# Norms between the first projections, one step-size chain for eight tokens, scans moved one projection forward

## What is computed

```python
h = rmsnorm(hidden_states, ln1_w)
zxbcdt = h @ w_in.T                       # z 512, xs 128, B 128, C 512, dt 4 columns
z, xs, Bs, Cs, dt = split(zxbcdt)
xBC = silu(causal_conv4(concat(xs, Bs, Cs)) + conv_b)
dt = softplus(dt + dt_bias)               # the step size, 4 heads
a = dt * -exp(A_log)
Ldec = tril(exp(cumsum(a)[:, None] - cumsum(a)[None, :]))
att = (C @ B.T) * Ldec
Y = att @ (xs * dt) + D * xs              # one chunk of 128 positions, state starts at 0
out = hidden + (Y * silu(z)) @ w_out.T    # then rmsnorm, MLP, and the other blocks
```

## Time and profile before

| | us |
|---|---|
| median of 3 runs | 1008.77 |
| lowest, highest | 1008.63, 1014.3 |
| the profiled execution as a whole | 1011.68 |
| its span in the profile | 1009.8 |
| PE busy | 966.8 |
| DVE, ACT, POOL busy | 571.8, 496.7, 403.9 |

### The profile page before, as it was taken

How to read it: one execution, slowest core, us unless ns; L and a number is a source line. 1 busy time by engine, 2 the same in 40 slices (tenths; PEclk the granted TensorE clock), 3 DMA queues, 4 the chain that set the end, 5 groups by cost and what they waited for, 6 DMA issues and landing times.

```text
span 1009.8 us, 15358 instructions
## 1 busy us (share of the span) xinstructions
PE 966.8 (96%) x5010; PEld 806.4 (80%) x5010; DVE 571.8 (57%) x1338; ACT 496.7 (49%) x1374; POOL 403.9 (40%) x341
## 2 busy tenths in 40 slices
PE   5999899999999999899999999999999999999894
PEld 3866488878888887788888888888888888888781
DVE  3665553422221266666666666566666666666766
ACT  4655342422231346455655654655555555655455
POOL 4334633744343453342442532622623514523312
PEclk9999999999999999899999999999999999999997
DMA  6200013310111111010020020020010110100002
GB/s 217 82 3 32 11 52 118 105 63 0 62 62 62 61 45 55 22 48 38 21 83 0 21 83 0 21 83 0 28 76 0 62 42 1 61 0 0 1 1 84
DMA packets 12976, 45.60 MB, mean 45 GB/s; under 512 B 1616, under 2 KB 2256, under 8 KB 9872
## 3 DMA queue, kind: packets, MB, share of 16 engines
q1 hardware_dynamic: 12944, 45.20, 12.9%
HBM read 43.10 MB, written 2.10 MB: 45 GB/s over the span
## 4 chain that ended last, share of the span: by engine, by line
PE 86%; DVE 5%; POOL 3%; ACT 3%; issue 2%; DMA 1%; SPq 0%; DVEq 0%; ACTq 0%; POOLq 0%
PE bank L373 25%; PE bank L374 24%; PE bank L375 24%; PE bank L651 6%; PE bank L661 3%; PE bank L384 1%; POOL res L1430 1%; DVE cbuf L1630 1%; DVE bst L1767 1%; PE bank L638 1%; POOL h_lo L1321 1%; DMA res<-in_x 1%; PE bank L452 1%; DVE xn L1590 0%; POOL rstd L1325 0%
## 5 line engine op out<-in xcount | busy, mean ns | idle before, releaser
L373 PE MATMUL bank<-act_hi,w_hi 128*128 128x512 f32 x560 | 225.0, 402 | 2.0 <-DVE act_lo L1577 1.6
L374 PE MATMUL bank<-act_lo,w_hi 128*128 128x512 f32 x560 | 220.1, 393 | 0.0
L375 PE MATMUL bank<-act_hi,w_lo 128*128 128x512 f32 x560 | 220.0, 393 | 0.0
L1501 POOL TENSOR_TENSOR pb<-pb,prec 128x512 f32<-128x512 f32 x64 | 66.6, 1040 | 313.2 <-DVE prec L1902 313.2
L1156 ACT ACTIVATE pb<-pb,nmax 128x128 f32<-128x128 f32 x256 | 99.8, 391 | 77.6 <-DVE nmax L1897 77.6
L373 PEld LDWEIGHTS bank<-act_hi,w_hi 128*128 128x128 f32 x560 | 106.0, 189 | 25.6 <-issue 4.3
L375 PEld LDWEIGHTS bank<-act_hi,w_lo 128*128 128x128 f32 x560 | 106.1, 189 | 22.9
L374 PEld LDWEIGHTS bank<-act_lo,w_hi 128*128 128x128 f32 x560 | 106.2, 190 | 22.6 <-issue 1.4
L373 PE MATMUL bank<-w_hi,ot_hi 128*128 128x512 f32 x256 | 105.5, 412 | 0.8 <-DVE res L1915 0.8
L375 PE MATMUL bank<-w_hi,ot_lo 128*128 128x512 f32 x256 | 101.1, 395 | 0.0
L374 PE MATMUL bank<-w_lo,ot_hi 128*128 128x512 f32 x256 | 100.7, 393 | 0.0
(11 more groups left out here) (189 smaller groups left out, 2068.2 us busy)
## 6 DMA issues: line engine op xcount, KB each, us to landing
raw_a<-in_w_q SPq DMA_DIRECT2D x8, 1024.0 KB, 4.7
raw_b<-in_w_o SPq DMA_DIRECT2D x8, 1024.0 KB, 4.7
raw_a<-in_w_gu SPq DMA_DIRECT2D x7, 1024.0 KB, 5.2
raw_b<-in_w_kv SPq DMA_DIRECT2D x8, 512.0 KB, 3.3
raw_b<-in_w_dn SPq DMA_DIRECT2D x7, 512.0 KB, 3.5
res<-in_x SPq DMA_DIRECT2D x8, 256.0 KB, 6.3
raw_b<-in_ctx_t SPq DMA_DIRECT2D x8, 256.0 KB, 3.0
xre<-in_x SPq DMA_DIRECT2D x2, 1024.0 KB, 7.0
```

The source lines that it names most:

```text
L373: mm(o, l_hi, r_hi, start=first, stop=False)
L374: mm(o, l_hi, r_lo, start=False, stop=False)
L375: return mm(o, l_lo, r_hi, start=False, stop=last)
L1501: TT(pb[:, jj % 2, :, :], pb[:, jj % 2, :, :], prec[:, jj % 2, :].unsqueeze(2).to_broadcast([P, GH, L]), ALU.mult).then_inc(p_norm, 1)
```

## The change

1. **Norms of tokens 4 to 7.** `norm_t(4)` to `norm_t(7)` stood before `in_step(6)` to `in_step(9)` and now stand before `in_step(1)` to `in_step(4)`; `dt_step(1)` comes behind `in_step(4)`, before `in_step(5)` (it stood behind `in_step(9)`). ACT, DVE and POOL get their steps of these norms earlier; on POOL `diag_d` moves behind `win_rest(7)`.
2. **One step-size chain.** `dt_row` holds all 1024 positions, `sp` all 32 columns. There is one `dt_turn` with eight transposes, one `dt_in`, one `dt_exp`, one `dt_out`, on 128x32 elements for 128x16. `decay_in(b)` waits for this one chain.
3. **Scans earlier.** `ssm1` is split into `cum_step` (the sum along the positions) and `xs_step` (transposition and scores), in this order. All scans stand one projection earlier on PE; for tokens 4 to 7 the `cum_step`s stand among `in_step(15)` to `in_step(19)`. On DVE `att_mul(b)` comes ahead of a `conv`, `y_out(b - 1)` behind it, and for tokens 4 to 7 `add_res`, `rms_var` and `rms_x` come behind an `att_mul` and `y_out`. ACT and POOL follow (`decay(4)` and (5) before `in_evac(16)`, `decay(6)` and (7) ahead of `gu_hi(0, 1)`).

The core of the diff, PE's list first:

```diff
                 if f == 12:
-                    pe.wait_ge(dt_a, 2)
+                    pe.wait_ge(dt_a, 1)
...
                 if n:
-                    pe.wait_ge(dt_a, 1)
+                    pe.wait_ge(dt_ev, 1)
...
-            def dt_turn(n):
-
-                pe.wait_ge(dt_ev, n + 1)
-                for j in range(HALF):
-                    t = nc.tensor.transpose(bank[6][:, j * NH:(j + 1) * NH], dt_row[:, j * L:(j + 1) * L],
+            def dt_turn():
+
+                pe.wait_ge(dt_ev, 2)
+                for b in range(B):
+                    t = nc.tensor.transpose(bank[6][:, b * NH:(b + 1) * NH], dt_row[:, b * L:(b + 1) * L],
                                             ident[0:NH, 0:NH])
                 t.then_inc(dt_t, 1)
 
-            def ssm1(b):
+            def cum_step(b):
+
+                pe.wait_ge(md_done, b + 1)
+                pe.wait_ge(*((exp_done, b) if b else (n_lo, 8)))
+                mm(bank[2][:, :], strict, md[:, b % 2, :, :], start=True, stop=True).then_inc(cum_mm, 1)
+
+            def xs_step(b):
...
+            def ssm1(b):
+
+                cum_step(b)
+                xs_step(b)
...
             in_step(0)
             dt_step(0)
-            in_step(1)
-            dt_turn(0)
-            for f in range(2, 6):
-                in_step(f)
             for i in range(4, 8):
                 norm_t(i, (bank[2], bank[3]))
-                in_step(i + 2)
+                in_step(i - 3)
             dt_step(1)
+            in_step(5)
+            dt_turn()
+            for f in range(6, 10):
+                in_step(f)
+            ssm1(0)
             in_step(10)
-            dt_turn(1)
-            ssm1(0)
+            ssm1(1)
             in_step(11)
-            ssm1(1)
-            in_step(12)
             ssm2(0)
             ssm1(2)
-            in_step(13)
+            in_step(12)
             ssm2(1)
             ssm1(3)
+            in_step(13)
+            ssm2(2)
             in_step(14)
-            ssm2(2)
+            ssm2(3)
+            cum_step(4)
             in_step(15)
-            ssm2(3)
+            cum_step(5)
             in_step(16)
             in_step(17)
+            xs_step(4)
             in_step(18)
+            xs_step(5)
+            ssm2(4)
+            cum_step(6)
             in_step(19)
-            ssm1(4)
             pe.wait_ge(conv_c, 2 * NCONV)
             out_step(0)
-            ssm1(5)
-            ssm2(4)
+            ssm2(5)
+            cum_step(7)
+            xs_step(6)
             out_step(1)
-            ssm1(6)
-            ssm2(5)
+            xs_step(7)
+            ssm2(6)
             out_step(2)
-            ssm1(7)
-            ssm2(6)
+            ssm2(7)
             out_step(3)
-            ssm2(7)
```

ACT, from the first scan to the second norm:

```diff
             conv_silu(6)
-            in_evac(12)
+            in_evac(11)
             conv_silu(7)
             x_evac(2)
             decay(2)
             y_split(0)
-            in_evac(13)
+            in_evac(12)
             x_evac(3)
             decay(3)
             conv_silu(8)
...
             gu_hi(0, 0)
+            decay(6)
+            y_split(4)
             square(8)
-            y_split(4)
+            decay(7)
             x_evac(6)
-            decay(6)
+            y_split(5)
             gu_hi(0, 1)
             square(9)
```

DVE:

```diff
+            rms_var(4)
+            rms_var(5)
+            rms_x(4)
             conv(0)
...
+            conv(2)
             norm_lo(6, nb)
-            dt_out(0)
+            conv(3)
             norm_lo(7, nb)
+            conv(4)
+            dt_in()
+            conv(5)
+            dt_out()
+            att_mul(0)
             conv(6)
-            dt_in(1)
-            att_mul(0)
+            att_mul(1)
             conv(7)
-            att_mul(1)
             y_out(0)
-            dt_out(1)
+            att_mul(2)
             conv(8)
-            att_mul(2)
             y_out(1)
+            att_mul(3)
             conv(9)
-            att_mul(3)
             y_out(2)
             conv(10)
             y_out(3)
             conv(11)
-            add_res(0, 0, OUT_BANK[0])
             att_mul(4)
-            rms_var(8)
             att_mul(5)
             y_out(4)
+            add_res(0, 0, OUT_BANK[0])
+            rms_var(8)
+            att_mul(6)
+            y_out(5)
             add_res(1, 1, OUT_BANK[1])
+            att_mul(7)
+            y_out(6)
             rms_x(8)
             rms_var(9)
-            att_mul(6)
-            y_out(5)
             add_res(2, 2, OUT_BANK[2])
+            y_out(7)
             rms_x(9)
             rms_var(10)
-            att_mul(7)
-            y_out(6)
             add_res(3, 3, OUT_BANK[3])
-            y_out(7)
```

More of the change, by code:

```diff
@@ L80, in build_program @@
             dt_sb = sb(m, "dt_sb", [P, B * NH])
-            sp = sb(m, "sp", [P, 7, HALF * NH])
+            sp = sb(m, "sp", [P, 7, B * NH])
             cbuf = sb(m, "cbuf", [P, 3, NTOK])
             xbc = sb(m, "xbc", [P, 2, NCONV, NTOK])
-            dt_row = sb(m, "dt_row", [NH, NTOK])
+            dt_row = sb(m, "dt_row", [NH, B * L])
             diag_d = sb(m, "diag_d", [P, NH, L])
@@ L436, in ssm1 @@
                 nc.tensor.transpose(bank[7][:, 0:P], xbc[:, n, 0, tok], ident).then_inc(xt_mm, 1)
-                pe.wait_ge(md_done, b + 1)
-                if b:
-                    pe.wait_ge(exp_done, b)
-                mm(bank[2][:, :], strict, md[:, b % 2, :, :], start=True, stop=True).then_inc(cum_mm, 1)
                 if b >= 2:
@@ L884, in dt_evac, with dt_exp @@
                 act.wait_ge(dt_mm, n + 1)
-                if n:
-                    act.wait_ge(dt_t, n)
-                A(dt_row[:, :], bank[6][0:NH, :], ACT.Copy).then_inc(dt_ev, 1)
-            def dt_exp(n):
-                act.wait_ge(dt_a, n + 1)
+                A(dt_row[:, n * NTOK:(n + 1) * NTOK], bank[6][0:NH, :], ACT.Copy).then_inc(dt_ev, 1)
+            def dt_exp():
+                act.wait_ge(dt_a, 1)
                 A(sp[:, 2, :], sp[:, 1, :], ACT.Exp).then_inc(dt_exp_done, 1)
@@ L965, in _ @@
             conv_silu(8)
-            in_evac(14)
+            in_evac(13)
             y_split(1)
             conv_silu(9)
-            in_evac(15)
-            conv_silu(10)
+            in_evac(14)
             y_split(2)
@@ L981, in _ @@
             wout_hi(1)
+            decay(4)
+            in_evac(15)
+            decay(5)
+            conv_silu(10)
             conv_silu(11)
@@ L987, in _ @@
             in_evac(17)
+            x_evac(4)
             in_evac(18)
+            x_evac(5)
             in_evac(19)
-            x_evac(4)
-            decay(4)
-            x_evac(5)
-            decay(5)
             tb = (bank[0], bank[1])
@@ L1338, in _ @@
             win_rest(1)
+            win_rest(2)
+            rsqrt(4)
+            win_rest(3)
+            rsqrt(5)
+            win_rest(4)
+            rsqrt(6)
+            win_rest(5)
+            rsqrt(7)
+            win_rest(6)
+            win_rest(7)
             pool.wait_ge(ld_small[5], 16)
@@ L1345, in _ @@
             TT(qk_w[:, :], chan_sb[:, nq:nq + 1], chan_sb[:, nq + 1:nq + 2], ALU.mult).then_inc(setup_p, 1)
-            for p in range(2, 6):
-                win_rest(p)
+            win_rest(8)
+            win_rest(9)
             def decay_in(b):
-                pool.wait_ge(dt_done, b // HALF + 1)
+                pool.wait_ge(dt_done, 1)
                 if b == 0:
@@ L1366, in y_rest @@
                 lo(y_lo[:, b % 4, :, :], yb[:, b % 2, :, :], y_hi[:, b % 4, :, :], ylo_done)
-            for i in range(4, 8):
-                rsqrt(i)
-                win_rest(i + 2)
             decay_in(0)
@@ L1384, in _ @@
             y_rest(0)
+            decay_in(4)
             decay_out(3)
             y_rest(1)
-            decay_in(4)
+            decay_in(5)
             y_rest(2)
@@ L1390, in _ @@
             wout_rest(1)
-            decay_in(5)
+            decay_out(4)
+            decay_out(5)
             y_rest(3)
@@ L1394, in _ @@
             wout_rest(3)
+            decay_in(6)
+            decay_in(7)
             def gu_rest(c, i):
@@ L1404, in dn_rest @@
                 lo(w_lo[:, s], raw_b[:, i * 512:(i + 1) * 512], w_hi[:, s], dn_l)
-            decay_out(4)
-            decay_in(6)
-            decay_out(5)
-            decay_in(7)
             gu_rest(0, 0)
+            decay_out(6)
             y_rest(4)
-            decay_out(6)
+            decay_out(7)
             rsqrt(8)
             y_rest(5)
-            decay_out(7)
             gu_rest(0, 1)
             rsqrt(9)
-            gu_rest(0, 2)
             y_rest(6)
             rsqrt(10)
+            gu_rest(0, 2)
             y_rest(7)
@@ L1645, in dt_in, with dt_out @@
                 V.tensor_copy(sp[:, 1, :], sp[:, 3, :]).then_inc(dt_a, 1)
-            def dt_out(n):
-                dve.wait_ge(dt_exp_done, n + 1)
+            def dt_out():
+                dve.wait_ge(dt_exp_done, 1)
```

(11 more changed lines are left out.)

55 lines of the change are left out of this document (25 added, 30 removed).

## The result

| | before | after | ratio |
|---|---|---|---|
| median of 20 runs, us | 1012.93 | 1009.29 | 0.9973 (95%: 0.9961 to 0.9986) |
| lowest to highest, us | 1006.27 to 1014.34 | 1005.73 to 1011.24 | |
| span of the profiled execution, us | 1009.8 | 1009.3 | |
| start of `norm_t(9)` in it, us | 130.54 | 127.15 | |

The change makes the kernel 0.27% faster, 2.7 us of 1010, with 1.4 to 3.9 us as the interval. (The executions come in steps, so the measure matters: the medians are 3.6 us apart, the means of the 20 runs 2.3 us.) I had forecast 4.0 us less (0.9961), so the direction and "within 1%" held and the size was too large. The absolute number fared worse: 1004.8 was counted from a median of three runs, 1008.77. Of the 20 runs of the kernel before, most lie near 1013 and a few near 1009 and 1006, and the three had drawn two of the lower kind.

A forecast was written before the change was run, and what follows sets the result against it. TensorE, busy for 96% of the span, was taken as the bound. Waits and lowered clock of 11.15 us, less 6.5 us remaining, plus 0.25, less 0.9 for the clock, gave 4.0 us: 1008.77 to 1004.8 us, range 1000.5 to 1009.5.

The forecast's parts named there:

- the sum of waits after the change: All TensorE waits expected in the edited part after the change: 1.0 + 4.7 + 0.8 = 6.5 us.
- the loop of part 3: In the scans, ssm2, att_mul, conv, y_out and back to ssm2 would take 5.5 us a token.
- the 11.15 us: Most the change could win by waits in the edited part: 8.85 us idle plus 2.3 us of lowered clock.
- Part 1, nothing won: Between the first projections, TensorE would wait 1.0 us before dt_step(1), where it had waited 0.9 + 0.26 us.
- The 0.25 us on PE: In the step-size chain, one dt_turn less saves 0.35 us, less 0.1 us for four more transposes.
- The waits of 0.2 and 0.6 us: In the tail, out_step(3) and out_step(4) would each wait for the add_res of a shared bank; 0.8 us together.
- The sum: Gain in the edited part before any clock cost: 11.15 - 6.5 + 0.25 = 4.9 us.
- The clock term of 0.9 us: Cost taken for TensorE's clock possibly falling in the new scan waits: 0.9 us, one fall costing 0 to 2.3 us.
- (c): Rival: in the tail the 4.76 us wait returns before out_step(3) or ssm2(7); about 1009 us, chance 0.13.
- (a): Rival: the scan loop does not bind, TensorE waits no longer than before between 71 and 85 us; 1001.6 us, chance 0.20.
- (b): Rival: the clock falls in the wait before cum_step(3) and stays down until ssm2(3); 1011 us, chance 0.13.
- (d): Rival: table switches ahead of cum_step(3) and cum_step(7) each cost 1.4 us more; 1007.6 us, chance 0.04.

The follow-up runs named there:

- e1: The changed kernel run again with no edit; ratio 0.9989 to the kernel before, mean 1009.1 us.
- e5: The kernel before with att_mul(7) and y_out(6) moved ahead of rms_x(9) and rms_var(10) on VectorE; ratio 0.9947 to the kernel before, mean 1006.7 us.
- e6: The changed kernel with all lists from the first scan on as in the kernel before; ratio 0.9973 to the kernel before, mean 1008.7 us.
- e2: The changed kernel with y_out directly behind att_mul, ahead of conv(7) and conv(8); ratio 0.9971 to the kernel before, mean 1009.1 us.
- e3: The changed kernel with x_evac(2) and decay(2) ahead of conv_silu(7) on ScalarE; ratio 0.9946 to the kernel before, mean 1006.4 us.
- e7: The changed kernel with GpSimd's y_rest(0) and y_rest(1) held until att_mul(2) and att_mul(3) are done; ratio 0.9954 to the kernel before, mean 1007.2 us.
- e4: The changed kernel with y_out directly behind att_mul and decay(2) ahead of conv_silu(7); ratio 0.9927 to the kernel before, mean 1004.6 us.

## Why the prediction was right and wrong

**The step that failed** is the sum of waits after the change, 6.5 us. It measured 7.8 us: the loop of part 3 was longer than priced (three waits of 5.3 us for 4.7), three small waits put at nothing came to 0.6 us, those of the tail to 1.05 us for 0.8, and the one before `dt_step(1)` to 0.85 for 1.0. With 0.1 us less from `dt_turn`, 3.4 us were won at `norm_t(9)` where 4.9 were forecast, and 1.9 us in e1, where the clock fell. Where PE waits, for what and in which order was right. Beside it two things outside the mechanism failed: the starting value of 1008.77 us, and the clock in the part that the change doesn't touch, which had no term. Details follow.

**What bounds, and the 11.15 us.** Right. The 4.76 us wait was `att_mul(7)` queued behind `rms_x(9)`, and its clock followed; e5 takes only that queueing away, and the wait shrinks to 1.64 us and the clock stays up. (The 2.3 us of clock were worked out with 0.97 us for `ssm2`, which the prices put at 0.87; 0.1 us.)

**Part 1, nothing won.** Right: the wait before `dt_step(1)` was 0.69 us (0.85 in starts) for the 1.0 forecast.

**Part 2.** The 0.25 us on PE was 0.12: `dt_turn` takes 0.58 us where two took 0.35 each, so the four more transposes cost 0.23 us for the 0.1 that I took, inside my bounds. That its larger effect was on VectorE (the second `dt_out` had made the waits of 1.47 and 0.32 us) I noted and then let part 3 overlay; e6 shows it alone.

**Part 3, the new bound.** The mechanism was right in each place and order: three waits, of 1.60, 1.10 and 2.15 us for 1.7, 1.15 and 1.8, with the releasers named; e2 and e3 remove them separately. The term that was mis-sized is the loop of 5.5 us: it was 5.97 us, because `att_mul`'s second instruction took 1.07 us for the 0.69 implied in 1.33. I had priced it at a place where GpSimd was idle; e7 shows that GpSimd's work beside it is the cause. The Trainium skill (GPSIMD Engine Reference, "1. Specifications") says that GpSimd's interfaces to SBUF, the scratchpad, are shared with VectorE, with contention where VectorE's instruction has two SBUF inputs. The trace agrees, 1.03 and 1.07 us against 0.69.

**Part 4.** Right in kind. The waits of 0.2 and 0.6 us were 0.23 and 0.44. Small waits that I took as nothing were not: `cum_step(5)` at 90.07 us, `cum_step(7)` at 109.56 us and `ssm2(7)` at 119.05 us each started 0.15 to 0.26 us late by the spacing of starts, 0.6 us together. Their rows:

```profile
90.07 1.10 PE L434 MATMUL bank<-md,cst 128*128 128x512 f32 x2
...
109.56 1.10 PE L434 MATMUL bank<-md,cst 128*128 128x512 f32 x2
...
119.05 1.10 PE L459 MATMUL bank<-att,xtok 128*128 128x512 f32 x2
```

**The sum.** At `norm_t(9)` I expected 4.9 us and got 3.4 (both executions at like start, 25.37 and 25.23 us). Of the 1.5 us missing, 0.6 are the three waits of part 3 (1.76 + 1.26 + 2.31 = 5.3 us in starts for 4.7), 0.6 the small waits, and 0.25 the two of the tail (1.05 us in starts for 0.8); the wait before `dt_step(1)` gave 0.15 back, `dt_turn` took 0.13, and 0.1 is not assigned.

**The clock term of 0.9 us.** Its size came out near, though it was chosen and not worked out: in the first profile it cost nothing, in e1 about 1.4 us (103.3 for 101.9), by the same wait of 2.1 us. The gain at `norm_t(9)` was 3.4 and 1.9 us in the two profiles, 2.6 us in the mean, near the 2.7 us of the result; two profiles are few for that. Waits of 2.57 us (e3) and 2.59 us (e2, e4) saw it fall, one of 2.36 us (e2, `cum_step(3)`) didn't, nor did 1.74 us (e7). The length of the wait alone doesn't decide.

**What I left out** is the same lottery in the 880 us that the change doesn't touch (2.8 us at the end alone, in the two profiles). I compared one span with a median of three and priced the clock only where I edited. The forecast of 4.0 us lies just outside the measured interval (1.4 to 3.9 us), and the absolute time was 4.5 us too low, for 4.2 us of which the drawn median of before (1008.77 for 1012.93) is the reason. Set against 1012.93 us, 1004.8 us would be 8.1 us less, and the medians moved by 3.6. That 1009.29 us still lies in my range is luck: its upper end of 1009.5 us came from rival (c), which did not happen.

**Rivals.** (a) fell: the loop binds. (b), the clock down from 73 to 85 us, was seen in no profile; it fell behind the last of the three waits when it fell. (c) fell. (d), the dearer table switch of the Trainium skill (ScalarE: Activation LUTs, "What ACT_TABLE_LOAD costs"), fell too: the load at 82.77 us in e4 is followed by its first exponential 1.29 us later, with no drain on ScalarE to be seen.

## What to carry to other kernels

In a queue written out by hand, ask of the longest wait which instruction stands ahead of the late one without being needed by it: here that (e5) took 4.3 us off the distance, and moving all the scans at most 1.5 us (changed against e6). When work is moved earlier, look at the shortest loop through all engines for what now stands inside it, since `conv` between `att_mul` and `y_out` cost 3 us at `ssm2(3)`, and each wait removed uncovered the next, so that the time did not move (e2). Differences under 1% need a look at where the bound engine's clock fell, far outside the edit too.
